# Cross-attention on one core: VectorE's low part put ahead of both maxima in each tile

## The reference

```python
query = hidden_states @ Wq          # (2, 1024, 640) @ (640, 640)
keyt = enc @ Wk                     # (2, 2044, 384) @ (384, 640)
valt = enc @ Wv
hs = _mha(query, keyt, valt)        # softmax(q k^T / sqrt(80)) v, 8 heads
...
ca_hs1 = _mha(ca_q1, residual, residual)
ca_q2 = ca_hs1 @ Wq
ca_hs2 = _mha(ca_q2, ca @ Wk_ca, ca @ Wv_ca)
out = (hs + ca_hs2) @ Wout + b_out + residual
```

## Time and profile before

| | us |
|---|---|
| median of 3 runs (1192.32 to 1192.5) | 1192.34 |
| profiled execution | 1192.6 |
| its span | 1190.8 |
| PE busy in the span | 1183.2 (99%) |
| DVE busy | 858.6 (72%) |
| ACT busy | 680.5 (57%) |
| POOL busy | 112.1 (9%) |

### The profile page before, as it was taken

How to read it: one execution, slowest core, us unless ns; L and a number is a source line. 1 busy time by engine, 2 the same in 40 slices (tenths; PEclk the granted TensorE clock), 3 DMA queues, 4 the chain that set the end, 5 groups by cost and what they waited for, 6 DMA issues and landing times.

```text
span 1190.8 us, 14961 instructions
## 1 busy us (share of the span) xinstructions
PE 1183.2 (99%) x5633; PEld 966.9 (81%) x5633; DVE 858.6 (72%) x1226; ACT 680.5 (57%) x797; POOL 112.1 (9%) x125
## 2 busy tenths in 40 slices
PE   9999999999999999999999999999999999999999
PEld 8888888788666677888888888888888888887998
DVE  7468625771144399989989989989899898986551
ACT  5323433222644477777777777777777777778210
POOL 1100000011000010100100110110110000000333
PEclk9999999999999999999999999999999999999999
DMA  8975785593920074364454445445436436421354
GB/s 314 353 272 178 258 309 204 219 340 98 298 62 1 1 184 116 80 143 111 96 128 111 110 114 124 114 97 140 105 89 161 107 75 159 135 68 56 105 206 143
DMA packets 140146, 178.08 MB, mean 150 GB/s; under 512 B 80729, under 2 KB 97881, under 8 KB 136234
## 3 DMA queue, kind: packets, MB, share of 16 engines
q1 hardware_dynamic: 132458, 156.34, 46.5%
q10 hardware_dynamic: 4752, 10.55, 2.6%
q0 software_dynamic: 2864, 10.24, 2.6%
HBM read 113.66 MB, written 63.28 MB: 149 GB/s over the span
## 4 chain that ended last, share of the span: by engine, by line
PE 95%; DVE 2%; DMA 1%; ACT 1%; issue 1%; SPq 0%; DVEq 0%; ACTq 0%
PE at_ps L1339 28%; PE bank L732 20%; PE at_ps L1316 19%; PE at_ps L255 9%; PE acc_t_ps L1095 7%; PE at_ps L1530 6%; PE s_ps L1063 2%; PE bank L709 1%; DMA x_f<-in_xT 1%; DVE prob_lo L1189 1%; PE acc_t_ps L1074 1%; PE f_ps L255 1%; PE f_ps L1016 1%; PE f_ps L1026 0%; PE at_ps L1533 0%
## 5 line engine op out<-in xcount | busy, mean ns | idle before, releaser
L264 DVE TENSOR_REDUCE mpart<-at_ps 128x1 f32<-128x512 f32 x480 | 326.6, 685 | 53.1 <-PE at_ps L255 51.9
L1254 ACT ACTIVATE prob_hi<-at_ps 128x1024 fp32r<-128x1024 f32 (+1 forms) x256 | 263.7, 1030 | 173.1 <-PE at_ps L1316 171.1
L1189 DVE TENSOR_TENSOR prob_lo<-probs,prob_hi 128x1024 fp32r<-128x1024 f32 (+1 forms) x256 | 311.8, 1218 | 20.5 <-ACT probs L1259 20.4
L1339 PE MATMUL at_ps<-prob_hi,v 128*128 128x512 f32 x1024 | 313.8, 391 | 0.0
L1259 ACT ACTIVATE probs<-at_ps 128x1024 f32<-128x1024 f32 (+1 forms) x256 | 261.5, 1022 | 0.0
L1339 PEld LDWEIGHTS at_ps<-prob_hi,v 128*128 128x128 f32 x1024 | 192.1, 188 | 43.3 <-ACT x_hi_place L1268 1.9
L255 PE MATMUL at_ps<-a 128*128 128x512 f32 x480 | 187.4, 390 | 0.4 <-DVE mpart L264 0.4
L1316 PE MATMUL at_ps<-a 128*128 128x512 f32 x512 | 158.5, 391 | 0.9 <-ACT probs L1259 0.6
L1339 PE MATMUL at_ps<-prob_lo,v 128*128 128x512 f32 x512 | 157.9, 390 | 0.1
L1316 PE MATMUL at_ps<-b 128*128 128x512 f32 x512 | 157.8, 389 | 0.0
L1316 PEld LDWEIGHTS at_ps<-a 128*128 128x128 f32 x512 | 95.5, 188 | 22.4 <-issue 1.7
(11 more groups left out here) (153 smaller groups left out, 1339.6 us busy)
## 6 DMA issues: line engine op xcount, KB each, us to landing
v_hi_d<-v_t SPq DMA_DIRECT2D x16, 648.0 KB, 6.2
v_lo_d<-v_t SPq DMA_DIRECT2D x16, 648.0 KB, 8.1
v<-v_hi_d SPq DMA_DIRECT2D x16, 648.0 KB, 5.6
v<-v_lo_d SPq DMA_DIRECT2D x16, 648.0 KB, 7.2
k_hi_d<-out_hi SPq DMA_DIRECT2D x40, 256.0 KB, 4.9
k_lo_d<-out_lo SPq DMA_DIRECT2D x40, 256.0 KB, 6.1
a<-k_hi_d SPq DMA_DIRECT2D x16, 640.0 KB, 7.7
b<-k_hi_d SPq DMA_DIRECT2D x16, 640.0 KB, 11.4
```

Source lines behind the costliest of these rows:

```text
L264: dve.tensor_reduce(self.mpart[:, g % 2, qt, c:c + 1], at[:, 0:w], AX, ALU.max).then_inc(self.mx_done, 1)
L1189: eng.tensor_tensor(pl[n % PL][0:r, :], prob[n % PF][0:r, :], ph[n % PB][0:r, :].bitcast(F32), ALU.subtract).then_inc(sem, 1)
L1254: act.activation(ph[n % PB][0:r, :], s_ps[n % 2][0:r, :], ACT.Exp, scale=SCALE).then_inc(ph_done, 1)
L1339: mm = pe.matmul(wide[3][:, u], a[:, t, :], y[:, u * CH:(u + 1) * CH], start=t == 0 and m == 0, stop=t == KT - 1 and m == 2)
```

## The change

VectorE does no maximum ahead of the low part. In each iteration it first makes the low part of tile n + 1 and then reduces all pieces of the iteration, two in ordinary iterations and two or three in iterations 0 to 11.

```diff
 NORM_AT = (8, 9, 10, 11)
-SPLIT_AT = 1
+SPLIT_AT = 0
 SLOTS = (1, 2, 0, 3)
```

## The result

| | before | after |
|---|---|---|
| median, us | 1192.42 | 1206.30 |
| lowest to highest of 4 runs | 1192.32 to 1192.56 | 1206.25 to 1206.39 |
| span of the profiled execution | 1190.8 | 1204.4 |
| median of each of the 12 experiments' own runs of before | 1192.31 to 1192.39 | |

The ratio is 1.0117, with a 95% interval of 1.0105 to 1.0129: the change makes the kernel 13.9 us slower, where 1206.8 was predicted. The instructions are the same in number (14961) and TensorE's granted clock is 1.00 throughout.

A forecast was written before the change was run, and what follows sets the result against it. TensorE, busy 601.16 of 601.22 us over ordinary attention, was taken to set the pace. Head changes 14 x 0.93 = 13.0 plus iterations 0 to 11, 1.4, gave 14.4 on 1192.6: 1207.0, for a median 1206.8; range 1202.8 to 1210.8.

The forecast's parts named there:

- The mechanism and its place: Head changes: the first maximum stands behind a low part waiting for a late exponential, so TensorE stops at a piece, 14 times.
- The size of a stop: Head change: the score pair behind the waiting piece starts at 776.84 instead of 775.91, 0.93 us; bounds 0.7 to 1.1.
- The 1.07: Where a piece waits for a maximum: the slot behind it comes 1.07 us behind the maximum's start.
- The rhythm back after one tile: Tile behind a head change's stop: ordinary rhythm returns, neither giving the 0.93 us back nor adding to it.
- Nothing in an ordinary tile: Some 200 ordinary tiles: the new order costs zero, as VectorE is free before the next low part can start.
- The margin of 0.70 us: Ordinary tile: the next tile's first piece has its buffer free at + 2.47 and is due at + 3.17.
- Iterations 0 to 11: First iterations, some with three pieces: + 1.4 us, from 0.62 by tile 3 and 0.82 in tiles 3 to 11; bounds 0 to 3.
- The last head: Last head change (t = 15 of head 14): has no pieces and stays as it is.
- Rival B: Head changes: the first maximum is done in time, so not slower; 1191.3 to 1193.8, say 1192.3 us; chance 0.04.
- Rival C: Ordinary tiles: their margin goes too, six tiles in each of 14 heads at 0.2 us, 17 us more: 1223; chance 0.03.
- Rival D: First iterations do not settle: each of 8 tiles of three pieces costs 0.5 us more, 1210.8; chance 0.06.
- The rule from the Trainium skill: VectorE's queue: strict FIFO, taking no ready maximum ahead of a waiting low part; without it head changes would cost nothing.

The follow-up runs named there:

- removing it: The changed kernel, but with the first maximum kept ahead of the low part at t = 0 of heads 1 to 15: 1193.57 us.
- making it alone: The kernel before, with the new order only in the iteration with t = 0 of heads 1 to 15: 1206.15 us.
- its dose: The changed kernel, with ScalarE copying only 256 of each 512 columns of a head's result from head 2 on: 1201.07 us.
- the 0.82 and 1.25 us waits above: Scores waiting for the maxima's row in two kernels: two maxima ahead of every low part (1207.57 us); order of before, low part last at t = 11 (1218.52 us).
- the experiment of 1.14 us lateness: The changed kernel plus an extra VectorE reduction over 1024 columns ahead of the low part, in one ordinary tile of each of heads 0 to 14: 1214.80 us.
- the kernel with the ordinary tiles alone: The kernel before, with the new order in every iteration from 12 on except those with t = 0: 1192.47 us.
- a low part 1.9 us later in one tile of 16: The kernel before, with the low part behind the second maximum and three small operations in iterations with t = 11: 1218.52 us.

## Why the prediction was right

- **The mechanism and its place** were as predicted: 14 stops of TensorE at the first piece two tiles behind each t = 15, because a maximum stands behind a late low part. Shown by removing it (1193.57), by making it alone (1206.15) and by its dose (the exponential 0.43 us less late, 0.4 us less a head).
- **The size of a stop** was put at 0.93 and is 0.97 in the mean of the 14 (tiles of 3.68 to 3.72 for 2.72). The 1.07 from the maximum's start to the slot behind the piece came out as 1.08; the rest are matmuls at 0.23 to 0.24 instead of 0.227 in the slots behind it. Against that the changed kernel gives something back in each head, at the tile with t = 14, the first one whose scores use the row of maxima of the next head. The rows of this tile in the second head, first in the kernel before, then in the changed one:

```profile
500.81 2.75 SPq L243 DMA_DIRECT2D b<-mrow  x4
...
504.82 0.34 PEld L1316 LDWEIGHTS at_ps<-a 128*128 128x128 f32 x2
...
504.97 0.63 PE L1316 MATMUL at_ps<-a 128*128 128x512 f32 x2
```

```profile
502.50 2.75 SPq L243 DMA_DIRECT2D b<-mrow  x4
...
506.72 0.41 PEld L1316 LDWEIGHTS at_ps<-a 128*128 128x128 f32 x2
...
506.95 0.62 PE L1316 MATMUL at_ps<-a 128*128 128x512 f32 x2
```

  In the kernel before the weight load starts 4.01 us behind the row's first issue, which is the distance of every tile that plainly waits for the row (the 0.82 and 1.25 us waits above: 4.03 and 4.04 to the matmul), and only 0.15 ahead of its matmul; in the changed one the row leaves 0.29 earlier in its tile and the weight load has its ordinary 0.23. The tile lasts 2.77 (504.97 to 507.74) before and 2.72 after. Over the heads this gives back about 0.5 us, and 0.2 more in head 12 (counted from 0), where the row's third issue is late.

  So between the result copies of the first head and those of the fourteenth there are 1047.80 - 467.96 = 579.84 us against 1034.85 - 466.98 = 567.87: 11.97 for 13 stops, 0.92 each. The prediction took this gain at nothing (the last maximum of a head comes earlier too, and the row hangs on it). That 14 x 0.93 came so near is in part luck: each stop is 0.04 larger, and the row gives about as much back.
- **The rhythm back after one tile** held: 2.73 and 2.72 us in the two tiles behind a stop, and the experiment of 1.14 us lateness shows that it is paid once.
- **Nothing in an ordinary tile** held (1192.47). The margin of 0.70 us was 0.1 too wide: it is counted at the piece, but by the prediction's own 1.07 the slot behind the piece (due at + 3.40) has only 3.40 - (1.74 + 1.07) = 0.59, and 0.58 to 0.60 was measured. An ordinary tile of the changed kernel has the low part waiting 0.30 us for ScalarE and starting 0.59 behind the tile start (462.91 against 462.32; predicted 0.60).
- **Iterations 0 to 11** were put at 1.4. Tile 3 starts at 429.57 (predicted 429.64), tile 12 at 456.87 (predicted 457.0), 1.27 later than before; the steps were right tile by tile, but for the third tile of three pieces in a row (3.01 instead of 3.10). Then the small waits in tiles 12 to 15 of the kernel before (its tile 12 lasts 2.84 us), which I had left as they were, go, and 0.98 is left at the first head's result copies (467.96 against 466.98). In a kernel of their own these iterations cost 1.06.
- **The last head**, where I had nothing, gave back 0.28 us: the tile that waits for its row lasts 1086.33 - 1083.57 = 2.76 us instead of 1072.71 - 1069.67 = 3.04. The scores of head 15 wait 0.33 us for the row of maxima in the changed kernel, and the row leaves 0.3 us earlier in its tile, since the last maximum ends earlier.

With the spans: 0.98 up to the first head's copies (no stop yet, the first iterations alone), 11.97 in the 13 stops up to the fourteenth head's, 0.67 behind them (the last stop less the gain of the last head): 13.6 = 1204.4 - 1190.8. The prediction's 14.4 is 0.8 too high: about half from the first iterations, the rest from the earlier row. The experiments add up in the same way: 13.8 for the stops alone and 1.06 for the first iterations alone, less about 1.0 that the earlier row gives back (0.5 + 0.2 + 0.3), is 13.9.

Rival B fell by the 14 waits. Rival C (whose sum is 1223.6, not 1223) fell by the kernel with the ordinary tiles alone. Rival D fell by iterations 0 to 11 alone, 1.06 us. The rule from the Trainium skill, "Perfetto Trace Analysis", section "Tensor Engine Instruction (MATMUL, LD_WEIGHTS)", that VectorE is strictly first in, first out: the trace agrees, and much more clearly than in the kernel before. VectorE sat idle for 1.94 us ahead of the low part while a piece lay ready for the last 1.35 of it (from 468.64).

## What to carry to other kernels

An order that is free in the steady tile is decided in the tiles that differ: look for the one in which an input comes late, and ask what stands behind that wait in the same queue and who needs it. The cost there is lateness minus margin, where the margin is read from the steady tile's timeline; here both could be read to about 0.1 us before anything ran. Follow not only the queue that is reordered but every queue that is released by the moved instruction: a low part 1.9 us later in one tile of 16 held back GpSimd, then a store, then a DMA queued behind it, and cost twice what the change under study did.

## What the runs showed that was not expected

- A piece whose buffer comes free late starts 0.73 to 0.74 us behind the start of the maximum that frees it, and the slot behind it comes 0.34 later instead of 0.23, in every such case looked at (471.13, 471.87, 472.21; 470.21, 470.95, 471.29). So a stop costs 0.11 us beyond the wait itself. In the rows the late piece's weight load starts together with its matmul (both at 471.87, ordinarily 0.22 us ahead), and the next one 0.10 behind.
- The row of maxima takes 4.03 us from SyncE's first issue to the first scores that wait for it (501.93 to 505.96, 502.57 to 506.61, and 1068.68 to 1072.71 in the kernel before), of which its four issues take 2.75. This path has no margin in the kernel before: the weight load of these scores is 0.05 to 0.09 late in each head, and the last head's scores wait 0.6.
- The profile of the kernel before puts the 0.6 us wait of the last head's scores down to an exponential, since one ended at the same moment (1072.71); the row had left 4.03 us before. Moving only the maxima's end (by 0.18 us) shortened the wait from 0.61 to 0.45, and its releaser then reads as the DMA.
